# Products of a block's pairs added up in PSUM, with four VectorE joins for seven, sums of squares on VectorE and another order at both ends

## What is computed

```python
def _rfs(xw, ab, AB, gs):
    dot_products = jnp.einsum('...d,rd->...r', xw, ab[:, None] * gs)
    correction = (0.5 * jnp.sum(xw * xw, axis=-1))[..., None] * (ab * ab)
    return 1.0 / math.sqrt(NUM_RFS) * AB * jnp.exp(dot_products - correction)
weights = _rfs(input_weights, ab, AB, proj_matrix)
feats = _rfs(x, ab, AB, proj_matrix)
attn = jnp.einsum('bsr,or->bso', feats, weights)
x = _layernorm(x + attn)
real = jnp.einsum('bti,io->bto', x, jnp.cos(theta + theta_noise))
imag = jnp.einsum('bti,io->bto', x, jnp.sin(phi + phi_noise))
x = _layernorm(x + jnp.sqrt(real * real + imag * imag))
```

## Time and profile before

| | |
|---|---|
| median of 3 runs | 696.8 us (695.82 to 698.42) |
| the profiled execution | 696.49 us |
| its span, first to last instruction | 694.6 us |
| PE, DVE, ACT, POOL busy | 680.8, 600.3, 460.7, 203.1 us |
| PE's matmuls, granted clock | 3010, 0.995 of full speed |

### The profile page before, as it was taken

How to read it: one execution, slowest core, us unless ns; L and a number is a source line. 1 busy time by engine, 2 the same in 40 slices (tenths; PEclk the granted TensorE clock), 3 DMA queues, 4 the chain that set the end, 5 groups by cost and what they waited for, 6 DMA issues and landing times. The chain is left out here.

```text
span 694.6 us, 10270 instructions
## 1 busy us (share of the span) xinstructions
PE 680.8 (98%) x3010; PEld 562.1 (81%) x3010; DVE 600.3 (86%) x968; ACT 460.7 (66%) x694; POOL 203.1 (29%) x257
## 2 busy tenths in 40 slices
PE   9999999999999999999999999999999999999993
PEld 7888888878888888888888888888888888888782
DVE  5888899889898988889888888898888888887897
ACT  7777998395666748566674855757485675847256
POOL 5772304105041140503214050320405033050324
PEclk9999999999999999999999999999999999999997
DMA  8862031471826547182654708355380835535232
GB/s 309 236 137 61 16 121 62 113 205 40 215 80 147 156 112 205 31 215 87 131 171 103 214 21 220 92 123 179 92 225 15 209 108 121 181 66 132 62 90 92
DMA packets 179254, 90.23 MB, mean 130 GB/s; under 512 B 120992, under 2 KB 149664, under 8 KB 179232
## 3 DMA queue, kind: packets, MB, share of 16 engines
q1 hardware_dynamic: 177936, 87.61, 46.5%
q0 software_dynamic: 1152, 2.10, 1.8%
q10 hardware_dynamic: 144, 0.26, 0.1%
HBM read 58.46 MB, written 31.49 MB: 129 GB/s over the span
## 5 line engine op out<-in xcount | busy, mean ns | idle before, releaser
L484 POOL TENSOR_TENSOR plain_late<-plain_late 128x1024 f32<-128x1024 f32 x26 | 68.1, 2621 | 274.7 <-ACT plain_late L835 274.7
L1009 PE MATMUL token_ps<-W_hi,F_hi 128*128 128x512 f32 x256 | 99.7, 389 | 0.9 <-DVE plain_late L1622 0.9
L1011 PE MATMUL token_ps<-W_hi,F_lo 128*128 128x512 f32 x256 | 99.6, 389 | 0.0
L1010 PE MATMUL token_ps<-W_lo,F_hi 128*128 128x512 f32 x256 | 99.6, 389 | 0.0
L737 ACT ACTIVATE o_tile<-plain_late,shift,rstd 128x512 f32<-128x512 f32 x56 | 42.6, 809 | 63.3 <-POOL shift L501 54.0
L731 ACT ACTIVATE plain_late<-plain_late 128x1024 f32<-128x1024 f32 x28 | 29.7, 1062 | 74.7 <-POOL plain_late L484 73.3
L1622 DVE TENSOR_TENSOR plain_late<-token_ps,plain_late 128x512 f32<-128x512 f32 x108 | 71.5, 682 | 3.9
L835 ACT ACTIVATE plain_late<-plain_late 128x1024 f32<-128x1024 f32 x54 | 55.2, 1056 | 19.0 <-DVE plain_late L1622 18.6
L623 ACT ACTIVATE F_hi<-plain_expo,ab 128x512 fp32r<-128x512 f32 x62 | 44.6, 720 | 31.6 <-DVE plain_expo L1253 31.5
L1121 PE MATMUL token_ps<-T_hi,zT_hi 128*128 128x512 f32 x162 | 63.1, 390 | 0.4 <-DVE zT_lo L1248 0.4
L1122 PE MATMUL token_ps<-T_lo,zT_hi 128*128 128x512 f32 x162 | 63.0, 389 | 0.0
(11 more groups left out here) (309 smaller groups left out, 1767.3 us busy)
## 6 DMA issues: line engine op xcount, KB each, us to landing
x_tok<-in_x SPq DMA_DIRECT2D x16, 1024.0 KB, 6.0
out_tokens<-o_tile SPq DMA_DIRECT2D x62, 256.0 KB, 3.1
plain_xT_lo<-in_xT SPq DMA_DIRECT2D x14, 1024.0 KB, 8.8
turned_pair<-plain_late SPq DMA_DIRECT2D x104, 128.0 KB, 3.0
plain_zT_lo<-turned_pair SPq DMA_DIRECT2D x27, 256.0 KB, 2.8
plain_zT_lo<-turned_pair SPq DMA_DIRECT2D x54, 128.0 KB, 2.8
norm_bc<-token_norms SPq DMA_DIRECT2D x15, 256.0 KB, 3.1
plain_T_hi<-in_gsT SPq DMA_DIRECT2D x4, 256.0 KB, 4.3
```

The costliest lines, as they stand in the source:

```text
L484: pool.tensor_tensor(parts[:, p, :, 0, :], parts[:, p, :, 0, :], parts[:, p, :, 1, :], ALU.add).then_inc(sum_made, 2)
L1009: nc.tensor.matmul(o, F_hi[:, c, cols], W_hi[:, c, :], start=(c == 0), stop=False)
L1010: nc.tensor.matmul(o, F_hi[:, c, cols], W_lo[:, c, :], start=False, stop=False)
L1011: return nc.tensor.matmul(o, F_lo[:, c, cols], W_hi[:, c, :], start=False, stop=(c == C - 1))
```

## The change

1. **PSUM.** Four banks serve one pair and the other four the other pair (`BANKS`). M1, M6, M5 and M3 all go into one bank, "sum", each added to what lies there: it holds M1, then U, then W, then C12. ACT copies it out between them (`copy_first`, `copy_U`, `copy_W`) and squares C12 straight out of it (`square_sum`). M7, M2 and M4 have banks of their own. PE waits for `first_copied` before M6, for `U_copied` before M5 and for `W_copied` before M3.
2. **Joins.** DVE has four for a pair: V = U + M7, C11 = M1 + M2, C22 = W + M7, C21 = V + M4.
3. **Order of products.** `PAIRED_ORDER` puts M7 and M2 between M1 and M6, one product (M4) between M6 and M5, and M1 of pair 1 between M5 and M3 of pair 0.
4. **Sums of squares.** `pair_sum` leaves POOL; DVE does all of them.
5. **The end.** Block 14 is split so that its M3 (pair 0) lies behind the first `mix` of block 15, which now goes into the other four banks; the features' remainders are taken before the second pair's half sums; the statistics of the last four tiles are all DVE's (one was ACT's), and the order of the last tiles is new.
6. **The start.** ACT issues the four loads of `wT`, ahead of its first instruction; SP issues those of `gs`, then `xT_first` in four transfers with a semaphore each, then `xis`. DVE rounds the first quarter of `wT`.

```diff
-        QUARTER_PS = [
-            {"M1": m1, "M6": token_ps[1], "M7": token_ps[2], "M5": token_ps[3], "M2": project_ps[0], "M4": project_ps[1], "M3": turn_ps[0]}
-            for m1 in (token_ps[0], turn_ps[1])
-        ]
+        BANKS = [{"sum": four[0], "M7": four[1], "M2": four[2], "M4": four[3]} for four in (token_ps, wide_project_ps)]
...
-        JOIN_ORDER = ["U", "V", "C22", "W", "C11", "C21", "C12"]
+        JOIN_ORDER = ["V", "C11", "C22", "C21"]
...
 SP
-                sp.dma_start(z[:, c, :], by_chunk(wT)[:, c, :]).then_inc(wT_loaded[c], 16)
+            for c in range(C):
+                sp.dma_start(xT_first[:, c, :], xT_blocks[0][:, c, :]).then_inc(xT_first_loaded[c], 16)
...
 POOL
-                    pair_sum(b - 1, 1)
                 pair_scale2(b - 1, 0)
                 pair_scale2(b - 1, 1)
                 make_damp(b, mv_made)
-                pair_sum(b, 0)
                 pair_residual2(b, 0)
...
 PE
+            def one_product(b, p, name, bank, his=pair_hi, los=pair_lo):
+
+                s = 2 * (b - PLAIN) + p + 1
+                if name == "M1":
+                    pe.wait_ge(halves_lo_made, s)
+                if name == "M7":
+                    pe.wait_ge(half_sums_lo_made, s)
+                if name == "M6":
+                    pe.wait_ge(first_copied, s)
+                if name == "M5":
+                    pe.wait_ge(U_copied, s)
+                if name == "M3":
+                    pe.wait_ge(W_copied, s)
+                quarter_product(BANKS[bank][name if name in ("M7", "M2", "M4") else "sum"][:, :],
+                                half(p, LEFT[name], his, los), RIGHT[name], name not in OPENS)
...
 ACT, step
-                for j in range(C):
-                    sum_square(b + 3, j, slot, 1 - slot)
+                sum_square(b + 3, 0, slot, 1 - slot)
+                sum_square(b + 3, 1, slot, 1 - slot)
+                copy_W(b, 0, 0, first)
+                sum_square(b + 3, 2, slot, 1 - slot)
+                copy_first(b, 1, 1, second)
+                load_table(ACT.Sqrt)
+                square_second(b, 0, first)
+                square_sum(b, 0, 0, first)
+                copy_U(b, 1, 1, second)
...
 DVE, step
+                join_V(b, 0, 0, first)
+                join_C11(b, 0, 0, first)
+                join_C22(b, 0, 0, first)
+                join_C21(b, 0, 0, first)
+                join_V(b, 1, 1, second)
+                pair_sum(b, 0)
+                join_C11(b, 1, 1, second)
+                turn_norms(b + 3, 1 - slot)
+                join_C22(b, 1, 1, second)
+                join_C21(b, 1, 1, second)
```

More of the change, by code:

```diff
@@ L260, in build, with joins_done, quarters_done, pair_squared @@
         SUMS_ORDER = ["T1", "T3", "T2", "T4"]
-        def joins_done(b, p, order, *names):
-            return 2 * JOINS * (b - PLAIN) + JOINS * p + JOIN_CREDIT + max(order.index(name) for name in names) + 1
+        def joins_done(b, p, name):
+            return 2 * JOINS * (b - PLAIN) + JOINS * p + JOIN_ORDER.index(name) + 1
+        def quarters_done(b, p, name, alone=False, split=False):
+            before_block = 2 * QUARTERS * (b - PLAIN)
+            if alone:
+                return before_block + QUARTERS * p + ALONE_ORDER.index(name) + 1
+            return before_block + (SPLIT_ORDER if split else PAIRED_ORDER).index((p, name)) + 1
+        def pair_squared(b, p):
+            return 2 * C * b + C * p + C + SQUARE_CREDIT
         NORMS_ON_PE = 2
@@ L569, in _ @@
             act.sem_inc(square_done, SQUARE_CREDIT)
+            for c in range(C):
+                act.dma_start(z[:, c, :], by_chunk(wT)[:, c, :]).then_inc(wT_loaded[c], 16)
             def sum_square(q, j, slot, k):
@@ L879, in last_steps @@
+                square_second(e, 0, first)
+                square_sum(e, 0, 0, first, split=True)
                 pair_roots(e, 0)
-                copy_first(e, 1)
+                copy_first(e, 1, 0, second, alone=True)
                 norm2(e, 0)
                 norm2(e, 1)
+                copy_U(e, 1, 0, second, alone=True)
+                copy_W(e, 1, 0, second, alone=True)
                 round_halves(b, 0, last_hi, last_raw)
                 round_half_sums(b, 0, last_hi, last_raw)
-                copy_first(b, 0)
@@ L892, in last_steps @@
-                square_tile(b, 0, 1)
-                square_tile(b, 0, 0)
+                copy_W(b, 0, 1, first, alone=True)
+                square_joined(b, 0, first, "C11")
+                square_second(b, 0, first)
+                square_sum(b, 0, 1, first, alone=True)
+                copy_first(b, 1, 0, last_parts, alone=True)
                 def root_tile(p, i, made, n):
@@ new lines, in own_product, with bank_joined @@
+            def own_product(b, p, name):
+                if name in OPENS:
+                    if p == 0:
+                        pe.wait_ge(y_made, C * b + OPENS.index(name) + 1)
+                    else:
+                        pe.wait_ge(expo_made, C * (b + 2) + OPENS.index(name) + 1)
+                one_product(b, p, name, p)
+            def bank_joined(b, p, name):
+                if name == "M1":
+                    pe.wait_ge(square_done, pair_squared(b, p))
+                else:
+                    pe.wait_ge(joined, joins_done(b, p, {"M7": "C22", "M2": "C11", "M4": "C21"}[name]))
@@ L1668, in open_step, with join_C21 @@
+            def join_C21(b, p, bank, place, **how):
+                dve.wait_ge(joined, joins_done(b, p, "V"))
+                dve.wait_ge(quarter_done, quarters_done(b, p, "M4", **how))
+                tt(place[:, 1, 0, :], BANKS[bank]["M4"][:, :], place[:, 1, 0, :], ALU.add).then_inc(joined, 1)
             def open_step(b, pair, slot, behind_plain=False):
```

385 lines of the change are left out of this document (163 added, 222 removed).

## The result

The changed kernel takes 703.7 us (median of 6, 702.91 to 705.69), the kernel before 696.8: a ratio of 1.010, 95% interval 1.0086 to 1.0113. It is 1.0% slower where I forecast 693.5 us. The profiled execution has a span of 701.6 us, 7.0 more than before.

What follows compares the result with a forecast made beforehand. PE, full in blocks 3 to 13, was the bound, so only the ends could gain: 696.49 − 0.87 (start) − 0.5 (blocks 14 and 15) − 1.86 (end) = 693.3, with the median 693.5 us; range 691.3 to 697.5.

Steps and rivals of the forecast that it cites:

- the sentence on DVE in the steady blocks: Blocks 3 to 13: pair 0's sum of squares delays DVE about 0.5 us, absorbed by 7 idle us; term 0.
- The gates of ACT's copies: M6, M5 and M3 wait for ACT copies: margin 0.43 us with one product between; loss 0, bounds 0 to 0.3 a block.
- the slower rival: PE waits for ACT at gates with one product between: one such gate a block gives 702 us, two 710; chance 0.12.
- the place that I had called the tightest: Pair 0's W copy behind two `sum_square`: done 9.15, needed 9.36, margin about 0.2 less hand-overs, 0.16 us.
- Small stalls in each block: W copy misses its 0.16 us by 0.1 to 0.35, with restarts, in twelve blocks: 694.8 to 697.7 us; chance 0.15.
- Loads: Steady blocks: DVE from 35.4 to 33.8 us a block, ACT from 26.6 to about 29.3, of 40.80.
- The table load: ACT's 1.28 us load in each block: no drain behind it, term 0; with a drain, 697 us, chance 0.03.
- Blocks 14 and 15: −1.15 us for the wait ahead of `mix`, +0.35 at M7, +0.3 at M6: −0.5, bounds −1.15 and +0.3.
- The end: From PE's last data to the last `normalise`: 7.14 us becomes 5.28, −1.86; bounds −2.2 and −1.1.
- The start: Up to block 0's first `project`: PE's wait for `xT_lo` and a short earlier one go, −0.87 us; bounds −1.2 and +0.3.
- The DMA engines are full: Rival at the start: it gives nothing, as the DMA engines are full; 694.3 to 695.3 us, chance 0.13.

Runs made afterwards that it cites:

- sum1_pool: The changed kernel with the sum of squares of pair 1 of the block before back on POOL: 696.5 us, ratio 0.999.
- sum0_early: The changed kernel with DVE's sum of pair 0 ahead of the join of V, and ACT's squares and roots reordered to suit: 696.8 us, ratio 0.9997.
- residual_dve: The changed kernel with pair 0's `pair_residual2` on DVE, behind the two subtractions of xT, not on POOL: 702.5 us, ratio 1.0070.
- residual_halves: The changed kernel with POOL's `pair_residual2` of pair 0 as two instructions of 512 columns, not one of 1024: 703.0 us, ratio 1.0082.
- best_early: The changed kernel with pair 0's sum ahead of the join of V, ACT's copies first at the end, and DVE's last joins ahead of statistics: 696.0 us.

## Why the prediction was wrong

**The step that failed** is the sentence on DVE in the steady blocks: that the sum of squares "delays what follows by about 0.5 us, which the 7 idle us of DVE's block absorb before PE wants `exponent`s", and so a term of 0. It failed in four ways.
- The deadline was the wrong one. Before M7 PE needs the remainders of the half sums; they had 1.44 us of slack, not 7. The idle time in a block's sum lies elsewhere: in the changed kernel 2.25 us stand ahead of V and 2.48 ahead of pair 1's half sums, in block 7.
- Both sums were counted in DVE's load, but only one as a delay. Pair 1's stands in the chain from statistics to half sums with its full 1.13 us. sum1_pool, which removes it, brings 40.80 back: shown.
- Pair 0's sum was placed by when its squares are done, not by what stands ahead of it in DVE's queue. The join of V waits there for the copy of U, and sum, roots, POOL's residual and the statistics follow from it. sum0_early changes only the order around it and cures as well: shown for the order as a whole.
- DVE's instructions were taken at the length that they have alone. Late as it is, POOL's residual meets the subtraction of xT and holds it for 1.37 us in each block.

How they add up can be read at two places of DVE's queue, both against the first matmul of the block they serve, blocks 4 to 13: the start of the residual of the second tile (L1381 before, L1399 now), in us ahead of it, and the end of the half sums' remainders, in us behind it, which PE needs at about 1.2:

| kernel | second residual, ahead | remainders made, behind | PE loses |
|---|---|---|---|
| before | 16.12 | −0.24 | 0 |
| sum of pair 0 earlier | 15.75 | −0.10 | 0 |
| sum of pair 1 on POOL | 14.73 to 15.09 | 0.57 to 0.91 | 0 |
| changed | 13.95 | 1.71 | 0.50 + 0.08 |

Without pair 1's sum DVE is up to 1.39 us late at the residual, without pair 0's delay 0.37, and both fit into 1.44. Together they are 2.17 late; 0.2 of it is absorbed by waits, 1.95 is left at the half sums, 0.50 over the slack.

POOL's hold is the larger part of what sum0_early wins (1.17 of 1.80). It isn't enough by itself: sum1_pool has it in full (2.59 for the first subtraction) and is as fast as before. But without it the changed kernel's remainders would come 1.95 − 1.37 = 0.6 us later than before, within the slack: an estimate, since the run that takes the hold away (residual_dve) puts 1.18 us of work in its place.

**The gates of ACT's copies**, on which the slower rival rested, held in the steady blocks. The only stall at one in blocks 2 to 14 of the changed kernel was M3 of pair 0 in block 5 (0.27 + 0.11), the place that I had called the tightest; but the copy stood behind a `sum_square` that waited 0.58 us for its load of x, which I hadn't counted. residual_dve and residual_halves show a few more, of up to 0.45 us, in blocks 3, 4 and 9. So slower came true by another mechanism than the rival's. "Small stalls in each block" had the shape of what happened, but named the wrong engine and was bounded at 0.35 a block, where it was 0.58.

**Loads.** DVE 34.1 and ACT 28.3 us a block in sum1_pool with one sum; in the changed kernel DVE 35.2, of which 1.37 are the hold: 33.8, as forecast. ACT (28.4 in the changed kernel) was forecast about 1.0 too high.

**The table load** has no drain behind it, here too: 361.47 to 362.75, and the next at 362.76 in ACT's timeline. The copy of pair 1's U behind it starts 0.04 us after PE's data in nine of blocks 3 to 13 and 0.4 us late in two, and PE isn't held at it. The drain that the Trainium skill names ("ScalarE: Activation LUTs", section "What ACT_TABLE_LOAD costs") would have made it late in every block, by the estimate in the prediction some 0.3 us.

**Blocks 14 and 15**: −0.5 forecast, +2.3 measured. The 1.15 ahead of `mix` was won. M6 of the last pair cost 1.9, where I took 0.3: I counted the squares ahead of the copy by their duration, not by what they wait for. M1 and M7 of block 15's pair 0 cost 0.84 together for the 0.35, its M3 0.20, and block 14 has the M7 stall (0.36) too.

**The end**: 7.14 to 5.00, −2.1 for the forecast −1.86. Right, and partly by luck: sum0_early, where PE stands as long at M6 of the last pair, has 5.00 too, and best_early, where that stall is gone, 6.05. PE came late, and DVE used PE's stall to clear its queue.

**The start**: −0.87 forecast, −0.2 measured by PE's block 2, which can't be told from nothing: in nine profiles with this start block 2 begins between 142.79 and 144.04, before at 143.12. The transfer wait went, but the first quarter of gs comes later (ACT rounds it at 4.40, before at 3.56), and DVE's remainder of it is held by POOL; PE lost 0.52 + 0.11 at 6.6. Curing that gave nothing, since PE waits for DVE in block 1. "The DMA engines are full" wasn't what decided: ACT began to round x at 11.69, before at 13.02.

## What to carry to other kernels

Measure slack at the deadline that comes first, by following the queue of the engine instruction by instruction to the operand that the bound engine takes next; the idle time in a block's sum says nothing about it. When work moves to a queue, ask of each instruction ahead of it what it waits for: here the one join ahead of a sum waited 2.25 us, and the one square ahead of a copy 1.76, where the moved sum itself takes 1.2. And add up all that comes late on one chain before comparing with its slack: taking away either of two delays brought the 7 us back.
